# A hybrid attention kernel: the key copy moves to ScalarE, the value product of the next sequence moves behind the next pair's first value products

## The chip, the cores and the metric

One core of one Trainium2 chip. The metric is the device time of one execution in microseconds (us); the median of three runs stands for the kernel. Engines: PE (TensorE, matmuls), DVE (VectorE), ACT (ScalarE), POOL (GpSimd), SP (SyncE, which here only issues DMAs). Each runs its own list of instructions in the order written; they meet at semaphores.

## The reference

`x` is 8 sequences of 512 tokens by 128 features, float32. Four steps, each with a residual:

```
x = x + attention_a(layernorm(x))     # 16 heads of 64, causal softmax
x = x + ffn(layernorm(x))
x = x + attention_b(layernorm(x))     # 16 heads of 64, causal softmax, then
                                      # y = y_in + heads @ Wo; layernorm(y) * gamma + beta
x = x + ffn(layernorm(x))
ffn: s = x @ Win + bin; g = sum over 16 of relu(s*W1 + b1)*W2, + b2; g @ Wout + bout
```

## The kernel before

Three parts follow one another. The front runs attention a and the first ffn for each sequence. Then come the **heads** (attention b), with the **back** (residual, normalization with gamma and beta, second ffn) of earlier sequences woven in. A drain ends it. The change is in heads and back.

The heads run over 8 sequences b and, in each, 8 pairs of heads p: 64 pairs, numbered n = 8b + p. A pair has three units: unit 0 is query blocks 0 and 1, unit 1 is block 2, unit 2 is block 3 (each with the keys up to its own block). A pair's code has three steps s = 0, 1, 2, and in step s each engine does what is due:

- PE (`heads_tensor`, L890): the scores of unit s (L842, and the mask with L847) into one of two wide PSUM buffers; the value products of one unit of an earlier pair (`pair_values`, L867 to L869) into bank CT. Step 0 also: the query projection of the next pair into bank QK, and the output product of pair n-3 (L886). Step 1 also: the key projection of the next pair into the same bank QK, and `context_turn_tensor` (L872), the transposes of pair n-2's context into bank MB. Step 2 also: the back's products, and `values_tensor` (L780), which makes one eighth of the next sequence's values, again in bank MB.
- DVE (`heads_vector`, L959): the row maxima of unit s (L969); the conversion of an earlier unit's probabilities to f16 (`split_vector`, L957); in step 0 the reciprocals, the scaled context (L983) and `values_vector` (L797), which writes `v_lo`, what the f16 values leave over; in step 1 `keys_vector` (L824), the copy of the keys out of QK. Then one of the eight adds of the ffn (L1108, the first of them L1104), and the back's norms.
- ACT (`heads_scalar`, L917): the exponentials of unit s (L933); step 0: the query copy (L818); step 1: `ctx_t` (L943), the turned context out of MB; step 2: `values_scalar` (L793), which writes `v_hi`. One ReLU of the ffn per pair (L1189).
- POOL (`heads_gpsimd`, L1012): the low half of each unit's probabilities (L1018), and small parts of the back. SP issues the DMAs that transpose the probabilities.

What must wait for what, around the change:

- `context_turn_tensor` of pair n-2, run in pair n, overwrites MB, so it waits until `v_lo` has been written n + 8 times (L876). The first 8 are made before the heads; pair n adds one.
- `values_tensor` waits for `ctx_t`, for the same reason.
- Unit 0's scores wait for `q_sb` and `k_sb`; the next pair's query projection waits for `k_sb`.
- The back of sequence c runs in sequence b = c + 1 (residual sum and statistics at p = 2, centering at p = 3, residual at p = 4, the turn at p = 6, the product with Win at p = 7), its eight ReLUs and adds in sequence c + 2, and its output product (L1172) after them. The back of sequence 6 is drawn together after the last pair (b = 8).

Of the kernel before, what the change touches and what calls it, by code (L numbers as in the profile page):

```python
# [35 lines left out]
NU = len(UNIT_ROWS)  # L36
# [12 lines left out]
def hybrid_kernel(nc, x_in, a_wq, a_wk, a_wv, a_wo, b_wq, b_wk, b_wv, b_wo, gamma, beta,  # L49
                  f_win, f_bin, f_w1, f_b1, f_w2, f_b2, f_wout, f_bout, out):  # L50
    B, S, D = x_in.shape
# [12 lines left out]
    with ExitStack() as ctx:  # L64
# [660 lines left out]
        DRAIN = 2 * HP + 2  # L725
# [5 lines left out]
        def unit_of_ffn(b, p, s):  # L731

            if b == B:
                return p * NU + s if p < NU else None
            return p if s == 0 and 0 <= b - 2 < B else None

        def leaves(b, p):

            if b == B and p == 3:
                return B - 2  # L740
            return b - 3 if p == 0 and 0 <= b - 3 < B and b - 3 != B - 2 else None

        def pair_exists(b, p):

            return 0 <= HP * b + p < PAIRS
# [54 lines left out]
        def project_tensor(pe, b, p, parts, done):  # L800

            n = number(b, p)
            wait(pe, *(("k_sb", n) if done == "q_ps" else ("q_sb", n + 1)))
            if done == "q_ps" and p == 0:
                wait(pe, "g_xt", b - 1)
            if done == "q_ps" and p == 1:
                wait(pe, "g_s", b - 1)
            if done == "q_ps" and p == 2:
# [11 lines left out]
        def keys_vector(dve, b, p):  # L820
            n = number(b, p)
            wait(dve, "k_ps", n + 1)
            wait(dve, "s2", n - 1)
            dve.tensor_copy(k_sb[p % 2][:, :], QK).then_inc(sem("k_sb"), 1)  # L824
# [65 lines left out]
        def heads_tensor(pe, b, p):  # L890
            fresh = pair_exists(b, p)
            for s in range(NU):
                if fresh:
                    pair_scores(pe, b, p, s)
                old = earlier(b, p, 2 if s < LAG - NU else 1)
                if pair_exists(*old):
                    pair_values(pe, *old, (s - LAG) % NU)
                if s == 0:
                    if pair_exists(*later(b, p)):
                        project_tensor(pe, *later(b, p), wq_parts, "q_ps")  # L900
                    if pair_exists(*earlier(b, p, 3)):
# [12 lines left out]
                if s == 2 and b < B - 1:  # L914
                    values_tensor(pe, b, p)

        def heads_scalar(act, b, p):  # L917
            n = number(b, p)
            for s in range(NU):
                if s == 2 and p == 6 and 0 <= b - 1 < B:  # L920
                    back_xt_scalar(act, b - 1)
                if s == 2 and p == 7 and 0 <= b - 1 < B:
                    back_s_scalar(act, b - 1)
                if pair_exists(b, p):
# [34 lines left out]
        def heads_vector(dve, b, p):  # L959
            n = number(b, p)  # L960
            before = earlier(b, p, 1)
            for s in range(NU):
                if pair_exists(b, p):
# [7 lines left out]
                    last.then_inc(sem(f"m{s}"), 1)  # L971
                u = (s - 1) % NU
# [97 lines left out]
        def back_center_vector(dve, c, half):  # L1070
            wait(dve, "gy_mv", c + 1)
            for i in range(half * QB // 2, (half + 1) * QB // 2):
# [5 lines left out]
        def back_residual_vector(dve, c, half):  # L1078
            wait(dve, "g_c", 2 * c + 2)
            wait(dve, "gy_rstd", c + 1)  # L1080
            wait(dve, "x_beta", c + 1)
            wait(dve, "g_xb", c)
            for i in range(half * QB // 2, (half + 1) * QB // 2):
# [4 lines left out]

        def back_adds_vector(dve, b, p, s):

            if s == 0 and p == 0 and 0 <= b - 3 < B and b - 3 != B - 2:
                back_add_vector(dve, b - 3, J - 1)
            if b == B:
                j = unit_of_ffn(b, p, s)
                if j is not None and 0 < j <= J:
                    back_add_vector(dve, b - 2, j - 1)
            elif s == 0 and p > 0 and 0 <= b - 2 < B:
                back_add_vector(dve, b - 2, p - 1)
# [21 lines left out]
        def back_gpsimd(pool, b, p, u):  # L1120
# [3 lines left out]
            if p == 2 and u == 1:  # L1124
                wait(pool, "kept", 16 * B)
                wait(pool, "g_x", 2 * c)
# [5 lines left out]
            if p == 4 and u == 2:  # L1132
                wait(pool, "g_x", 2 * c + 2)
# [4 lines left out]
            if p == 5 and u == 0:  # L1138
# [3 lines left out]
            if p == 5 and u > 0:  # L1142
                if u == 1:
# [3 lines left out]
                for i in range((u - 1) * QB // 2, u * QB // 2):  # L1147
# [7 lines left out]
        def back_turn_tensor(pe, c):  # L1155
            wait(pe, "g_y", 2 * c + 2)
            wait(pe, "g_done", c if c == B - 1 else c - 1)
            wait(pe, "k_sb", bank_left(c + 1, 6))
            transposes(pe, QK, ffn_norm.tokens(), QB).then_inc(sem("g_xt_ps"), 1)

        def back_s_tensor(pe, c):
            wait(pe, "g_xt", c + 1)
            wait(pe, "k_sb", bank_left(c + 1, 7))
# [3 lines left out]
        def back_out_tensor(pe, c):  # L1167
            wait(pe, "g_add", J * c + J)
            wait(pe, "g_s", min(c + 2, B) if c != B - 2 else c + 1)
            wait(pe, "k_sb", bank_left(c + 3, 0))  # L1170
# [79 lines left out]
        def _(act):  # L1250
# [5 lines left out]
            queries_scalar(act, 0, 0)  # L1256
            over_pairs(act, heads_scalar)

        @block.vector
        def _(dve):  # L1260
# [5 lines left out]
            keys_vector(dve, 0, 0)  # L1266
# [26 lines left out]
```

## Time and profile before

| | |
|---|---|
| median of 3 runs | 909.11 us (909.02 to 909.72) |
| profiled execution | 910.46 us, span in the trace 908.7 us |
| heads, pairs 0 to 63 (trace) | from 239.15 us |
| granted PE clock, mean of the span | 0.919 of full speed |
| busy over the span | PE 81%, DVE 81%, ACT 60%, POOL 58% |

A busy time is the time in which an engine works on some instruction. Times in the trace count from the start of the span. What a change is worth is read inside the heads, from the start of one pair's scores on PE to the next one's.

### The profile page before, as it was taken

To read this page: it belongs to the slowest core of one execution; us is meant where nothing else is said; L and a number is where in the kernel's file an instruction comes from. 1 tells how busy PE (TensorE), PEld (TensorE's weight loads), DVE (VectorE), ACT (ScalarE), POOL (GpSimd) and SP (SyncE) were. 2 spreads that over 40 slices of the span, in tenths; PEclk is the share of its full clock that TensorE was granted. 3 is DMA by queue.
4 is the path that set the end of the run, shared out by engine and by line. 5 is a ranking of instruction groups with operands and counts; after the bars stand their busy time and mean duration, and the time that the engine had idled before them with its cause. 6 is when DMAs were issued, how large, how long until landed. Compare 5 with 4: busy or idle time off the path is not lost. (4 is left out here: it accounts for less than half of the span.)

```text
span 908.7 us, 21242 instructions
## 1 busy us (share of the span) xinstructions
PE 732.3 (81%) x7592; PEld 524.5 (58%) x7592; DVE 740.5 (81%) x1422; ACT 542.1 (60%) x1511; POOL 522.9 (58%) x496
## 2 busy tenths in 40 slices
PE   3476666641899999998899899889989998998852
PEld 2365555531557676675677567666756665675541
DVE  1478888864577789889989988998898899899973
ACT  0357666652466665675677567666756666765643
POOL 2146666443165666756756575676658566656831
PEclk9598878855799999999999999999999999999995
DMA  9111110101199987897789688888878887887740
GB/s 202 42 32 42 50 56 35 36 35 46 21 144 155 155 141 132 140 149 124 127 138 152 108 141 132 142 131 138 151 117 131 144 139 125 136 154 126 133 93 22
DMA packets 367142, 100.29 MB, mean 110 GB/s; under 512 B 347968, under 2 KB 364864, under 8 KB 367040
## 3 DMA queue, kind: packets, MB, share of 16 engines
q1 hardware_dynamic: 363776, 96.86, 61.6%
q10 hardware_dynamic: 3264, 2.10, 0.9%
q8 instruction: 60, 0.98, 0.5%
q14 instruction: 42, 0.34, 0.1%
HBM read 8.73 MB, written 2.10 MB: 12 GB/s over the span
## 5 line engine op out<-in xcount | busy, mean ns | idle before, releaser
L1018 POOL TENSOR_TENSOR prob_hl<-prob,prob_hl 128x768 f16<-128x768 f32 (+1 forms) x192 | 347.8, 1812 | 235.6 <-DVE prob_hl L957 235.6
L933 ACT ACTIVATE prob<-wide,neg_max 128x128 f32<-128x128 f32 (+3 forms) x512 | 264.5, 525 | 209.1 <-DVE neg_max L969 209.0
L969 DVE TENSOR_REDUCE neg_max<-wide 128x2 f32<-128x256 f32 (+3 forms) x256 | 203.6, 816 | 66.5 <-PE wide L847 65.0
L842 PE MATMUL wide<-k_sb,q_sb 64*128 64x128 f32 (+3 forms) x1024 | 190.8, 470 | 2.6 <-ACT prob L933 1.6
L867 PE MATMUL bank<-v_hi,prob_t 128*128 128x64 f16 x1280 | 132.2, 193 | 16.6 <-DMA prob_t<-prob_hl 8.8
L869 PE MATMUL bank<-v_hi,prob_t 128*128 128x64 f16 x1280 | 132.2, 193 | 0.0
L868 PE MATMUL bank<-v_lo,prob_t 128*128 128x64 f16 x1280 | 132.2, 193 | 0.0
L957 DVE CAST prob_hl<-prob 128x768 f16<-128x768 f32 (+1 forms) x192 | 126.4, 658 | 1.8 <-ACT prob L933 1.6
L867 PEld LDWEIGHTS bank<-v_hi,prob_t 128*128 128x128 f16 x1280 | 115.5, 98 | 20.5 <-issue 10.6
L869 PEld LDWEIGHTS bank<-v_hi,prob_t 128*128 128x128 f16 x1280 | 114.0, 98 | 0.0
L868 PEld LDWEIGHTS bank<-v_lo,prob_t 128*128 128x128 f16 x1280 | 113.8, 98 | 0.0
L933 ACT ACTIVATION_READ_ACCUMULATOR prob<-wide,neg_max 128x1 f32 x512 | 102.6, 200 | 0.0
L842 PEld LDWEIGHTS wide<-k_sb,q_sb 64*128 64x128 f32 x1024 | 72.4, 186 | 44.1 <-issue 35.7
L847 PEld LDWEIGHTS wide<-mask_bf,ident_bf 128*128 128x128 bf16 x512 | 29.1, 98 | 105.1 <-issue 105.1
L1108 DVE SCALAR_TENSOR_TENSOR ffn_g<-relu_two,w,ffn_g 128x512 f32<-128x512 f32 x56 | 87.6, 1563 | 1.8 <-ACT relu_two L1189 0.7
L886 PEld LDWEIGHTS bank<-wo_up,ctx_t 128*128 128x128 f32 x512 | 66.8, 191 | 6.1 <-ACT ctx_t L943 0.9
L886 PE MATMUL bank<-wo_up,ctx_t 128*128 128x128 f32 x512 | 67.7, 275 | 0.7 <-ACT ctx_t L943 0.7
L847 PE MATMUL wide<-mask_bf,ident_bf 128*128 128x128 bf16 x512 | 62.1, 224 | 0.0
L1189 ACT ACTIVATE relu_two<-ffn_s,b,w 128x512 f32<-128x512 f32 x64 | 52.7, 827 | 2.6 <-DVE ffn_g L1104 1.7
L410 ACT ACTIVATE v_hi<-ffn_s,b,w 128x512 f32<-128x512 f32 x64 | 51.2, 813 | 1.4 <-DVE ffn_g L417 0.4
L421 DVE SCALAR_TENSOR_TENSOR ffn_g<-v_hi,w,ffn_g 128x512 f32<-128x512 f32 x56 | 43.8, 783 | 5.6 <-ACT v_hi L410 4.2
L160 PE MATMUL bank<-wv_b_hi,xt_hi 128*128 128x512 f32 x62 | 32.5, 524 | 18.7 <-ACT ctx_t L943 16.6
(190 smaller groups left out, 1474.6 us busy)
## 6 DMA issues: line engine op xcount, KB each, us to landing
prob_t<-prob_hl SPq DMA_TRANSPOSE x384, 3.1
x_next<-in_L_attn_a_in_features SPq DMA_DIRECT2D x8, 256.0 KB, 3.1
x_attn<-in_L_attn_a_in_features SPq DMA_DIRECT2D x8, 256.0 KB, 3.0
x_sb<-x_done SPq DMA_DIRECT2D x8, 256.0 KB, 2.3
y_res<-bn_y SPq DMA_DIRECT2D x8, 256.0 KB, 2.3
out_x<-x_done SPq DMA_DIRECT2D x8, 256.0 KB, 2.7
wq_a<-in_L_attn_a_w_q ACTq DMA_DIRECT2D x1, 512.0 KB, 5.3
wq_b<-in_L_attn_b_Wq SPq DMA_DIRECT2D x1, 512.0 KB, 8.3
```

Source lines behind the costliest of these rows:

```text
L842: pe.matmul(dst[:, h, c:c + m], q[e, i * P:(i + 1) * P], k[e, 0:m], start=(i == UNIT_ROWS[u][0]), stop=False)
L847: last = pe.matmul(dst[:, h, c:c + P], ident_bf[:, :], mask_bf[:, :], start=False, stop=(i == UNIT_ROWS[u][-1]))
L867: pe.matmul(dst, prob_t[u][:, h * m + k, :], hi, start=(j == 0), stop=False)
L868: pe.matmul(dst, prob_t[u][:, h * m + k, :], lo, start=False, stop=False)
L869: last = pe.matmul(dst, prob_t[u][:, (2 + h) * m + k, :], hi, start=False, stop=(j == i))
L886: last = pe.matmul(YA[:, i * P:(i + 1) * P], ctx_t[:, i * P:(i + 1) * P], wo_up[:, p, :], start=(p == 0 and i == 0), stop=(p == HP - 1 and ...
L933: last = act.activation(prob_2[s][:, at:at + m], score_banks(p, s)[:, h, c:c + m], ACT.Exp, bias=neg_max[p % 2][:, h, i:i + 1], accum_out= ...
L957: dve.tensor_copy(prob_hl[u][:, 0:w], prob_2[u][:, 0:w]).then_inc(sem(f"ph{u}"), 1)
L969: last = dve.tensor_reduce(neg_max[p % 2][:, :, i:i + 1], score_banks(p, s)[:, :, c:c + m], AX.X, ALU.max, negate=True)
L1018: pool.tensor_tensor(prob_hl[u][:, w:2 * w], prob_2[u][:, 0:w], prob_hl[u][:, 0:w], ALU.subtract)\
L1108: dve.scalar_tensor_tensor(out=ffn_g[:, :], in0=relu_two[:, j % 2, :], scalar=w2_2[:, j:j + 1], in1=ffn_g[:, :], op0=ALU.mult, op1=ALU.add ...
L1189: act.activation(relu_two[:, j % 2, :], ffn_s[:, :], ACT.Relu, bias=b1_2[:, j:j + 1], scale=w1_2[:, j:j + 1]).then_inc(sem("g_relu"), 1)
```

## The change

Five things, all in heads and back.

1. `keys_vector` on DVE becomes `keys_scalar` on ACT, in step 1 behind the `ctx_t` copy.
2. `values_tensor` of pair n moves from the end of step 2 to step 0 of pair n+1, behind the first value products and before the query projection. `values_scalar` follows it to step 0 of pair n+1, behind the exponentials; `values_vector` goes from step 0 to step 1 of pair n+1, behind the conversion.
3. The ffn's ReLUs and adds move by one pair (the add of step 0 goes to step 1 of the next pair) and, on DVE, in front of the conversion.
4. Centering and residual aren't halved any more; each is done at once, in step 2 of p = 3 and p = 4, before the conversion. The statistics behind them, the moments and POOL's parts move back by one or more steps.
5. The turn, the product with Win and the output product of the back move back by one pair each, and the drain has one more pair.

```
-        DRAIN = 2 * HP + 2
+        DRAIN = 2 * HP + 3
...
+        def relu_at(b, p, s):
+
+            if b == B and p > 0:
+                k = (p - 1) * NU + s
+                return (B - 2, k) if k < J else None
+            c, j = (b - 2, p - 1) if p > 0 else (b - 3, J - 1)
+            return (c, j) if s == 0 and 0 <= c < B and c != B - 2 else None
+
+        def adds_at(b, p, s):
+
+            found = []
+            c, j = (b - 2, p - 2) if p > 1 else (b - 3, J - 2 + p)
+            if s == 1 and 0 <= c < B and c != B - 2:
+                found.append((c, j))
+            k = (p - 1) * NU + s
+            if b == B and 0 < k <= J:
+                found.append((B - 2, k - 1))
+            return found
...
-        def keys_vector(dve, b, p):
+        def keys_scalar(act, b, p):
             n = number(b, p)
-            wait(dve, "k_ps", n + 1)
-            wait(dve, "s2", n - 1)
-            dve.tensor_copy(k_sb[p % 2][:, :], QK).then_inc(sem("k_sb"), 1)
+            wait(act, "k_ps", n + 1)
+            wait(act, "s2", n - 1)
+            act.copy(k_sb[p % 2][:, :], QK).then_inc(sem("k_sb"), 1)
```

In `heads_tensor`:

```
                 if s == 0:
+                    bv, pv = earlier(b, p, 1)
+                    if 0 <= bv < B - 1:
+                        values_tensor(pe, bv, pv)
                     if pair_exists(*later(b, p)):
                         project_tensor(pe, *later(b, p), wq_parts, "q_ps")
...
-                if s == 2 and p == 6 and 0 <= b - 1 < B:
+                if s == 2 and p == 7 and 0 <= b - 1 < B:
                     back_turn_tensor(pe, b - 1)
-                if s == 2 and p == 7 and 0 <= b - 1 < B:
-                    back_s_tensor(pe, b - 1)
+                if s == 2 and p == 0 and 0 <= b - 2 < B:
+                    back_s_tensor(pe, b - 2)
                 if s == 2 and leaves(b, p) is not None:
                     back_out_tensor(pe, leaves(b, p))
-                if s == 2 and b < B - 1:
-                    values_tensor(pe, b, p)
```

In `heads_scalar`:

```
+                if s == 0:
+                    bv, pv = earlier(b, p, 1)
+                    if 0 <= bv < B - 1:
+                        values_scalar(act, bv + 1, pv, MB)
                 if s == 0 and pair_exists(*later(b, p)):
                     queries_scalar(act, *later(b, p))
                 if s == 1 and pair_exists(*earlier(b, p, 2)):
...
-                if s == 2 and b < B - 1:
-                    values_scalar(act, b + 1, p, MB)
-                j = unit_of_ffn(b, p, s)
-                if j is not None and j < J:
-                    back_relu_scalar(act, b - 2, j)
+                if s == 1 and pair_exists(*later(b, p)):
+                    keys_scalar(act, *later(b, p))
```

In `heads_vector`, behind the maxima:

```
+                for c, j in adds_at(b, p, s):
+                    back_add_vector(dve, c, j)
+                if s == 2 and p == 3 and 0 <= b - 1 < B:
+                    back_center_vector(dve, b - 1)
+                if s == 2 and p == 4 and 0 <= b - 1 < B:
+                    back_residual_vector(dve, b - 1)
                 u = (s - 1) % NU
                 if pair_exists(*(before if s == 0 else (b, p))):
                     split_vector(dve, *(before if s == 0 else (b, p)), u)
...
-                if s == 0:
+                if s == 1:
                     bv, pv = before
                     if 0 <= bv < B - 1:
                         values_vector(dve, bv + 1, pv, MB)
-                if s == 1 and pair_exists(*later(b, p)):
-                    keys_vector(dve, *later(b, p))
-                back_adds_vector(dve, b, p, s)
...
-                if s > 0 and p == 3 and 0 <= b - 1 < B:
-                    back_center_vector(dve, b - 1, s - 1)
-                if s < 2 and p == 4 and 0 <= b - 1 < B:
-                    back_residual_vector(dve, b - 1, s)
-                if s == 2 and p == 4 and 0 <= b - 1 < B:
-                    wait(dve, "g_x", 2 * b)
+                if s == 0 and p == 5 and 0 <= b - 1 < B:
+                    wait(dve, "g_x", b)
                     back_statistics(dve, ffn_norm, lambda i: x_ffn[:, i, :], "gf", b - 1)
-                if s == 0 and p == 5 and 0 <= b - 1 < B:
+                if s == 1 and p == 5 and 0 <= b - 1 < B:
                     back_moments(dve, ffn_norm, "gf", b - 1)
```

In `back_gpsimd` (POOL):

```
-            if p == 4 and u == 2:
-                wait(pool, "g_x", 2 * c + 2)
+            if p == 5 and u == 0:
+                wait(pool, "g_x", c + 1)
                 wait(pool, "g_done", c - 1)
...
-            if p == 5 and u == 0:
+            if p == 5 and u == 2:
                 back_rstd_gpsimd(pool, ffn_norm, "gf", c)
...
-            if p == 5 and u > 0:
-                if u == 1:
+            if p == 6 and u < 2:
+                if u == 0:
```

## Rows read from the trace of the kernel before

**Rows 1.** The page, busy us, share of the span and instructions of each engine.

```profile
PE 732.3 (81%) x7592; PEld 524.5 (58%) x7592; DVE 740.5 (81%) x1422; ACT 542.1 (60%) x1511; POOL 522.9 (58%) x496
```

**Rows 2.** Busy time by stretch: start:end, length, engines, PE clock, DMA share, GB/s.

```profile
282.69:291.62 8.93, 8.93 (x107) 6.30 (x106) 6.61 (x13) 5.84 (x19) 5.41 (x3) 1.00 0.98 146
465.30:546.26 80.96, 75.34 (x855) 52.57 (x854) 74.09 (x122) 53.42 (x163) 52.29 (x36) 1.00 0.80 134
584.82:596.62 11.80, 9.49 (x106) 6.43 (x105) 11.80 (x19) 6.55 (x20) 6.25 (x4) 1.00 0.71 113
798.28:856.28 58.00, 51.08 (x617) 36.00 (x617) 57.14 (x92) 36.28 (x114) 41.18 (x29) 1.00 0.82 136
856.28:908.70 52.42, 23.51 (x245) 16.95 (x244) 32.37 (x61) 23.08 (x44) 17.42 (x17) 0.74 0.35 69
```

**Rows 3.** Timeline of PE in pair 5: start us, us, instruction.

```profile
282.69 0.93 PE L842 MATMUL wide<-k_sb,q_sb 64*128 64x128 f32 x8
...
286.25 0.92 PE L842 MATMUL wide<-k_sb,q_sb 64*128 64x384 f32 x4
...
288.52 0.60 PE L194 MATMUL bank<-ident,ctx_sb 128*128 128x128 f32 x4
289.05 1.13 PE L842 MATMUL wide<-k_sb,q_sb 64*128 64x512 f32 x4
...
290.75 0.47 PE L160 MATMUL bank<-wv_b_hi,xt_hi 128*128 128x512 f32 x1
```

**Rows 4.** PE groups, 465.3 to 546.26: busy us, mean ns of one, idle before.

```profile
L1172 PE MATMUL bank<-wout,ffn_g 128*128 128x128 f32 x8 | 1.1, 285 | 0.0
L1164 PE MATMUL bank<-x_attn,win 128*128 128x512 f32 x2 | 1.1, 634 | 0.0
L194 PE MATMUL bank<-ident,fn_y 128*128 128x128 f32 x4 | 0.6, 279 | 0.7 <-DVE k_sb L824 0.7
```

**Rows 5.** PE's waits, 465.3 to 546.26: us in total, times, longest.

```profile
PE bank L160 <- ACT ctx_t L943: 3.2, 3, 1.4
PE bank L867 <- DVE ctx_sb L983: 1.0, 1, 1.0
```

**Rows 6.** Timeline of DVE in pair 5.

```profile
286.19 0.68 DVE L797 TENSOR_TENSOR v_lo<-bank,v_hi 128x512 f16<-128x512 f32 x1
287.42 0.96 DVE L969 TENSOR_REDUCE neg_max<-wide 128x2 f32<-128x768 f32 x1 [0.55 <-PE wide L847]
288.30 0.55 DVE L957 CAST prob_hl<-prob 128x768 f16<-128x768 f32 x1
288.76 0.69 DVE L824 COPY k_sb<-bank 128x512 f32<-128x512 f32 x1
...
291.57 0.55 DVE L957 CAST prob_hl<-prob 128x768 f16<-128x768 f32 x1
```

**Rows 7.** Timeline of ACT in pair 5.

```profile
288.41 0.58 ACT L933 ACTIVATE prob<-wide,neg_max 128x384 f32<-128x384 f32 x1 [1.16 <-DVE neg_max L969]
...
289.54 0.58 ACT L943 COPY ctx_t<-bank 128x512 f32<-128x512 f32 x1
```

**Rows 8.** Timeline of DVE, three of the ffn's adds and the instruction behind one.

```profile
611.65 2.22 DVE L1108 SCALAR_TENSOR_TENSOR ffn_g<-relu_two,w,ffn_g 128x512 f32<-128x512 f32 x1
...
631.32 1.58 DVE L1108 SCALAR_TENSOR_TENSOR ffn_g<-relu_two,w,ffn_g 128x512 f32<-128x512 f32 x1
...
881.11 0.74 DVE L1108 SCALAR_TENSOR_TENSOR ffn_g<-relu_two,w,ffn_g 128x512 f32<-128x512 f32 x1
881.77 0.87 DVE L1053 BATCH_NORM_STATS2 yn_stats<-y_res 128x6 f32<-128x128 f32 x4
```

**Rows 9.** Timeline of POOL beside the first two adds, and a unit of 768.

```profile
611.18 2.14 POOL L1018 TENSOR_TENSOR prob_hl<-prob,prob_hl 128x1024 f16<-128x1024 f32 x1
...
615.28 1.64 POOL L1018 TENSOR_TENSOR prob_hl<-prob,prob_hl 128x768 f16<-128x768 f32 x1 [0.67 <-DVE prob_hl L957]
...
630.22 2.14 POOL L1018 TENSOR_TENSOR prob_hl<-prob,prob_hl 128x1024 f16<-128x1024 f32 x1 [1.64 <-DVE prob_hl L957]
```

**Rows 10.** Timeline of PE, the start of pair 3.

```profile
264.84 0.93 PE L842 MATMUL wide<-k_sb,q_sb 64*128 64x128 f32 x8
```

More of the change, by code:

```diff
@@ L729, in hybrid_kernel @@
         y_norm = Norm("yn", ln_b_eps, applied=False)
[L731 to L735, printed above, removed]
+        def relu_at(b, p, s):
[13 more added lines that the diff above has]
+            return found
         def leaves(b, p):
-            if b == B and p == 3:
+            if b == B and p == 4:
                 return B - 2
-            return b - 3 if p == 0 and 0 <= b - 3 < B and b - 3 != B - 2 else None
+            return b - 3 if p == 1 and 0 <= b - 3 < B and b - 3 != B - 2 else None
         def pair_exists(b, p):
@@ L803, in project_tensor @@
             wait(pe, *(("k_sb", n) if done == "q_ps" else ("q_sb", n + 1)))
-            if done == "q_ps" and p == 0:
+            if done == "q_ps" and p == 1:
                 wait(pe, "g_xt", b - 1)
-            if done == "q_ps" and p == 1:
+            if done == "q_ps" and p == 2:
                 wait(pe, "g_s", b - 1)
-            if done == "q_ps" and p == 2:
+            if done == "q_ps" and p == 3:
                 wait(pe, "g_done", b - 2)
@@ L919, in heads_scalar @@
             for s in range(NU):
[L920 to L923, printed above, removed]
                 if pair_exists(b, p):
@@ L943, in heads_scalar @@
                     act.copy(ctx_t[:, :], MB[:, :]).then_inc(sem("ctx_t"), 1)
-                if s == 2 and b < B - 1:
-                    values_scalar(act, b + 1, p, MB)
-                j = unit_of_ffn(b, p, s)
-                if j is not None and j < J:
-                    back_relu_scalar(act, b - 2, j)
+                if s == 1 and pair_exists(*later(b, p)):
+                    keys_scalar(act, *later(b, p))
+                if s == 2 and p == 7 and 0 <= b - 1 < B:
+                    back_xt_scalar(act, b - 1)
+                if s == 2 and p == 0 and 0 <= b - 2 < B:
+                    back_s_scalar(act, b - 2)
+                if relu_at(b, p, s) is not None:
+                    back_relu_scalar(act, *relu_at(b, p, s))
         def split_vector(dve, b, p, u):
@@ L1068, in back_rstd_gpsimd, with back_center_vector @@
                 .then_inc(sem(f"{done}_rstd"), 1)
-        def back_center_vector(dve, c, half):
+        def back_center_vector(dve, c):
             wait(dve, "gy_mv", c + 1)
-            for i in range(half * QB // 2, (half + 1) * QB // 2):
+            for i in range(QB):
                 last = dve.scalar_tensor_tensor(out=y_gb[:, i, :], in0=y_res[:, c * QB + i, :],
@@ L1076, in back_center_vector, with back_residual_vector @@
             last.then_inc(sem("g_c"), 1)
-        def back_residual_vector(dve, c, half):
-            wait(dve, "g_c", 2 * c + 2)
+        def back_residual_vector(dve, c):
+            wait(dve, "g_c", c + 1)
             wait(dve, "gy_rstd", c + 1)
             wait(dve, "x_beta", c + 1)
-            wait(dve, "g_xb", c)
-            for i in range(half * QB // 2, (half + 1) * QB // 2):
+            wait(dve, "g_y", 2 * c)
+            for i in range(QB):
                 last = dve.scalar_tensor_tensor(out=x_ffn[:, i, :], in0=y_gb[:, i, :],
@@ L1087, in back_residual_vector @@
             last.then_inc(sem("g_x"), 1)
[L1089 to L1098, printed above, removed]
         def back_add_vector(dve, c, j):
@@ L1125, in back_gpsimd @@
                 wait(pool, "kept", 16 * B)
-                wait(pool, "g_x", 2 * c)
+                wait(pool, "g_x", c)
                 pool.tensor_tensor(x_beta[:, :, :], x_sb[:, seq(c), :],
@@ L1146, in back_gpsimd @@
                     wait(pool, "g_xt_ps", c)
-                for i in range((u - 1) * QB // 2, u * QB // 2):
+                for i in range(u * QB // 2, (u + 1) * QB // 2):
                     last = pool.tensor_scalar(ffn_norm.y[:, i, :], x_ffn[:, i, :], ffn_norm.neg_mean[:, i:i + 1],
@@ L1157, in back_turn_tensor @@
             wait(pe, "g_done", c if c == B - 1 else c - 1)
-            wait(pe, "k_sb", bank_left(c + 1, 6))
+            wait(pe, "k_sb", bank_left(c + 1, 7))
             transposes(pe, QK, ffn_norm.tokens(), QB).then_inc(sem("g_xt_ps"), 1)
@@ L1162, in back_s_tensor @@
             wait(pe, "g_xt", c + 1)
-            wait(pe, "k_sb", bank_left(c + 1, 7))
+            wait(pe, "k_sb", bank_left(c + 2, 0))
             pe.matmul(QK[:, :], win2[:, :, :].rearrange("p a m -> p (a m)"), ffn_xt, start=True, stop=True)\
@@ L1168, in back_out_tensor @@
             wait(pe, "g_add", J * c + J)
+            wait(pe, "g_done", c)
             wait(pe, "g_s", min(c + 2, B) if c != B - 2 else c + 1)
-            wait(pe, "k_sb", bank_left(c + 3, 0))
+            wait(pe, "k_sb", bank_left(c + 3, 1))
             for i in range(QB):
@@ L1256, in _ @@
             queries_scalar(act, 0, 0)
+            keys_scalar(act, 0, 0)
             over_pairs(act, heads_scalar)
@@ L1265, in _ @@
                 values_vector(dve, 0, k, VB[k % len(VB)])
-            keys_vector(dve, 0, 0)
             over_pairs(dve, heads_vector)
```

## Prediction

> **What bounds the kernel now.** I read the page's busy shares first. PE and DVE are level at 81% of the span, ACT and POOL far below [rows 1]. That leaves open which one sets the time, so I cut the heads part (B) into stretches. Pair 5 lasts 8.93 us, PE is busy for all of it and DVE for only 6.61. A whole sequence in the middle (pairs 24 to 31) lasts 80.96, with PE 75.34 and DVE 74.09; pair 36 alone lasts 11.80, with DVE busy for all of it and PE for 9.49 [rows 2]. So there are two regimes: PE sets the time where DVE has only the pair's own work, and DVE sets it where a normalization of the back part falls.
>
> How much each is worth comes from PE's own order. Pair 5 starts at 282.69, pair 6 at 291.62, with no gap [rows 2, 3]: 8.93 us is PE's floor for a pair that also makes a value product. Eight of them are 71.4 us. The three back-end products of a sequence take 0.6, 1.1 and 1.1 us [rows 4], about 0.2 of each overlapping its neighbours: 2.3 us. The remaining 80.96 - 71.4 - 2.3 = 7.3 us per sequence are waits, the largest of them PE's wait for `ctx_t` (3.2), behind which DVE's lateness stands [rows 5].
>
> **What a pair looks like on PE.** Call T the start of unit 1's scores, 286.25. The context turn starts at T+2.27, unit 2's scores at T+2.80, the value product at T+4.50, and the next pair at T+5.37; so the value product costs 0.87 [rows 2, 3]. On DVE the maximum of unit 1 starts at T+1.17, the conversion of unit 0 at T+2.05, and the instruction behind it (now the key copy) at T+2.51 [rows 6].
>
> **Part 1: the key copy goes from DVE to ACT.** DVE loses 0.69 us per pair, 0.6 of which counts, because starts overlap the end before by 0.08. ACT gains a copy of 0.58 [rows 6, 7]. ACT is busy for 53.42 of 80.96 [rows 2], so it has the room. Its order matters more: the copy stands behind unit 1's exponentials (T+2.16) and the `ctx_t` copy (T+3.29) [rows 7]. Without any other wait it ends at about T+3.29+0.46+0.58 = T+4.33; the next scores start at T+4.50 now that the value product isn't before them. Cost nothing, with a cover of 0.2 us.
>
> **Part 2: the value product goes from the end of pair n to step 0 of pair n+1.** PE's work is the same. The wait for `ctx_t` that stood in front of it is now met long before it. But the product writes bank MB, and the context turn of step 1 writes MB too. The turn waits for `v_lo` number n + 8, which is the second half of exactly this product: DVE must have subtracted it before PE may turn. Before, that subtraction was in DVE's step 0, over at 286.87 [rows 6], 1.65 us ahead of the turn (288.52). The diff moves it to step 1, behind the maximum of unit 1, the add and the conversion of unit 0.
>
> So a new chain closes inside each pair: unit 1's scores, maximum, add, conversion, `v_lo`, turn. Without an add, `v_lo` takes the slot of the key copy: it starts at T+2.51, takes 0.68 [rows 6], ends at T+3.19, and PE resumes some 0.03 later, at T+3.22 in place of T+2.27. Stall: **0.95 us**. Unit 1's maximum can't start earlier, because it waits for PE. Behind the turn PE has unit 2's scores, and then everything up to the next unit 1, all in order, so nothing gives the stall back. DVE was the late one before and has no fault here: even when it is free, the chain is longer than PE's 2.27.
>
> **Part 3: the adds.** From sequence 2 on each pair has one add, now between maximum and conversion, so it lengthens the same chain. What it costs there must be chosen. In its place of now it takes 1.58 or 2.22 [rows 8]. Both times it ends 0.54 us after the POOL subtraction that runs beside it (630.22+2.14 = 632.36 against 632.90; 611.18+2.14 = 613.32 against 613.87) [rows 8, 9]. It stands still while POOL works. With POOL idle it takes 0.74, and the next instruction starts after 0.66 [rows 8]. Is POOL idle at the new place? The conversion of unit 1 ends at 291.57+0.55, 3.07 after unit 2's scores start (289.05); the next pair S starts 1.70 after those scores, so that is S+1.37 [rows 3, 6]. POOL's subtraction (1.64) runs to S+3.06; a conversion of unit 2 held back until then ends some 0.55 later, and POOL's 2.14 for unit 2 are over by about S+5.8 [rows 9]. The add comes at T+2.05 with T = S+3.56+0.87, so at S+6.5. It clears POOL by 0.7 us. I take 0.66: the stall is 0.95 + 0.66 = **1.61 us**. The other end is 1.58, a stall of 2.45.
>
> **Part 4: center and residual in one piece each, statistics and moments a step later.** They stay on DVE, which now has 0.6 us less per pair for the key copy, 0.8 less for the add and a longer pair. I cost them at nothing on DVE. They do push POOL's work later, so that in three or four pairs of eight POOL still runs when the add comes. By the rows of the add this is 0.3 to 0.8 us each time; I take 1.2 us per sequence, 6 in all (bounds 0 and 16).
>
> **The sum.** Pairs 3 to 56 last from 264.84 to 798.28, 533.4 us [rows 2, 10]. PE's floor in them is 53 x 8.93 + 8.06 (pair 56 makes no value product) = 481.4, the back-end products 12.4; waits 39.6, and these go. Pair 56 gains a value product (+0.87), one output product leaves the stretch (-0.9). Stalls: pairs 3 to 17, 15 x 0.95 = 14.3; pairs 18 to 56, 39 x 1.61 = 62.8. Together -39.6 + 77.1 = **+37.5**. Pairs 0 to 2: one stall more, one value product less, +0.1. POOL in the way: +6. Pairs 57 to 62 have no value product and no stall; they last 58.00, DVE 57.14 of it [rows 2], while PE needs 6 x 8.06 + 0.9 = 49.3. DVE is relieved, but in pairs this short the cover of 0.2 us for the key copy goes with each late maximum: I take 3 us for that, **-5.7** (bounds -8.7 and -3). Tail (52.42 [rows 2]): the turn of the last sequence moves in (+0.5), and the eight ReLUs of sequence 6 start one pair later, so their adds stand ahead of the last sequence's centering: **+3** (bounds 0 and 5). Sum: 37.5 + 0.1 + 6 - 5.7 + 3 = +40.9. The profiled execution took 910.46 and would take 951.4; the median of the runs is 909.11, so I forecast **950 us**.
>
> **Rivals.**
> 1. *DVE was the bound and its relief decides: faster.* For it: DVE is busy for 92% of a sequence (74.09 of 80.96) and PE loads weights for 52.57, 65% [rows 2]. If PE had room for the stall, the 39.6 us of waits and most of the 8.7 in the last pairs would go and nothing come back: about 865. Against it: pair 5 leaves PE no gap, and DVE's 6.61 don't explain its length. The point of decision is the stall: 39.6 + 5.7 over 55 pairs is 0.8 us; below that the kernel is faster. That needs `v_lo` by T+3.0, and without any add it comes at T+3.19. The Trainium skill (Perfetto Trace Analysis, Identifying the Most-Contended Engine) says that matmul busy time is no good measure for PE and that LDWEIGHTS busy is to be used; by it PE has a third of its time free and this rival would hold. I trust the gap-free pair more.
> 2. *The adds still run into POOL in every pair.* Then 39 x 0.84 = 33 us more: about 983. It needs POOL to be 0.7 us later than I worked out.
> 3. *The stall overlaps waits that I let vanish*, or is shorter because PE refills faster behind it: 915 to 934.
>
> **Chances.** Forecast's case (934 to 968) 0.78; rival 1 0.06; rival 2 0.08; rival 3 0.06; within 0.2%, what a measurement of this kernel can't tell from no change, 0.02. The low end of the range, 934, has no POOL cost, -8.7 in pairs 57 to 62 and nothing in the tail (938), and a stall shorter by 0.07. The high end, 970, has POOL's 16, -3, and 5 (966), and a stall longer by 0.07. Faster 0.06, same 0.02, slower 0.92.
>
> **What would show it.** In the profile after: pair 5 lasts 9.9 us and a middle pair 10.5 to 11, where both regimes were before; PE waits for `v_lo` in front of the context turn, 1 us without an add and 1.6 with one, 55 times, and no more for `ctx_t`; the add takes 0.75 in most pairs; DVE is busy for some 62 us of a sequence of 86. Pairs from 57 on last 8.1 to 9. Wrong would be: a turn that doesn't wait, adds of 1.6, or PE gaps before unit 0's scores (the key copy late on ACT).

## The result

The changed kernel takes 965.53 us (median of 4 runs, 964.21 to 967.33) against 909.07 for the kernel before: a ratio of 1.062 (95% interval 1.060 to 1.064). It is slower by 56 us; forecast were 950, with 934 to 970 as the range.

**The profile after.** The page's busy shares answer to [rows 1]:

```profile
PE 742.8 (77%) x7592; PEld 531.4 (55%) x7592; DVE 655.5 (68%) x1358; ACT 579.6 (60%) x1575; POOL 517.6 (54%) x496
```

DVE is relieved by 85 us, and the kernel is slower all the same. The stretches, in the columns of [rows 2]: pair 5, two pairs of sequence 3 (p = 4 and p = 5), pairs 32 to 39, pairs 57 to 62, the tail.

```profile
283.27:293.22 9.95, 9.05 (x108) 6.36 (x105) 6.62 (x11) 6.45 (x20) 5.42 (x3) 1.00 0.72 140
526.44:537.39 10.95, 9.36 (x109) 6.43 (x106) 8.71 (x16) 7.04 (x21) 5.43 (x3) 1.00 0.67 129
537.39:550.08 12.69, 10.91 (x108) 7.10 (x105) 9.69 (x24) 7.15 (x21) 6.64 (x4) 0.87 0.69 119
571.77:662.71 90.94, 78.15 (x856) 54.39 (x855) 60.78 (x115) 58.23 (x170) 51.47 (x35) 0.96 0.66 121
853.48:907.44 53.96, 51.13 (x621) 36.36 (x621) 44.34 (x86) 40.05 (x121) 37.84 (x25) 1.00 0.90 145
907.44:963.40 55.96, 25.38 (x251) 18.84 (x248) 34.04 (x62) 24.11 (x45) 20.17 (x21) 0.72 0.33 62
```

Pair 5 was 8.93 us with PE busy throughout; now it is 9.95 with PE busy for 9.05. A sequence was 80.96 with DVE busy for 74.09; now it is 90.94 with DVE busy for 60.78. Pairs 57 to 62, which have no value product, got shorter as a stretch (58.00 before). No engine is full, and that is the sign of a chain that runs over several engines. The granted clock, 1.00 before from pair 1 to the end of the heads, is below that in some pairs now (0.87 in the third row).

The chain itself, PE and then DVE in pair 5 (timeline):

```profile
287.52 0.92 PE L855 MATMUL wide<-k_sb,q_sb 64*128 64x384 f32 x4
...
290.86 0.63 PE L194 MATMUL bank<-ident,ctx_sb 128*128 128x128 f32 x4 [0.90 <-DVE v_lo L810]
291.42 1.13 PE L855 MATMUL wide<-k_sb,q_sb 64*128 64x512 f32 x4
```

```profile
288.69 0.96 DVE L986 TENSOR_REDUCE neg_max<-wide 128x2 f32<-128x768 f32 x1 [1.21 <-PE wide L860]
289.57 0.55 DVE L974 CAST prob_hl<-prob 128x768 f16<-128x768 f32 x1
290.04 0.68 DVE L810 TENSOR_TENSOR v_lo<-bank,v_hi 128x512 f16<-128x512 f32 x1
292.80 1.23 DVE L986 TENSOR_REDUCE neg_max<-wide 128x2 f32<-128x1024 f32 x1 [2.09 <-PE wide L860]
```

With T = 287.52: the maximum starts at T+1.17, `v_lo` at T+2.52 and ends at T+3.20, as in the prediction (T+1.17, T+2.51, T+3.19). The turn starts at T+3.34, not T+3.22: PE took 0.14 us to resume behind DVE, not the 0.03 that the forecast put there. DVE then sits idle for 2.09 us, waiting for PE. Neither engine is full: each waits for the other in every pair.

PE's waits from 263.39 to 853.48 (pairs 3 to 56), in all:

```profile
PE bank L194 <- DVE v_lo L810: 76.6, 54, 1.8
PE bank L880 <- DMA prob_t<-prob_hl: 0.3, 1, 0.3
```

54 waits in 54 pairs and hardly anything else; the wait for `ctx_t` of [rows 5] is gone. The adds, 571.77 to 662.71:

```profile
L1113 DVE SCALAR_TENSOR_TENSOR ffn_g<-relu_two,w,ffn_g 128x512 f32<-128x512 f32 x7 | 5.5, 784 | 0.0
```

They take 0.78 us on the average, against 1.81 in the same pairs before. That is a mean: 0.74 in most pairs, 1.05 where POOL still runs beside the add (p = 3).

### The profile page after: what moved, and what is told of

The parts are those of the page before. It is cut to its first block and busy times, and to the rows that moved or that the text cites. A ratio compares the mean times of both kernels' runs of the same rounds, so it can differ in the third digit from the quotient of the medians.

```text
span 963.4 us, 21234 instructions
## 1 busy us (share of the span) xinstructions
PE 742.8 (77%) x7592; PEld 531.4 (55%) x7592; DVE 655.5 (68%) x1358; ACT 579.6 (60%) x1575; POOL 517.6 (54%) x496
## 5 line engine op out<-in xcount | busy, mean ns | idle before, releaser
L855 PE MATMUL wide<-k_sb,q_sb 64*128 64x128 f32 (+3 forms) x1024 | 195.7, 481 | 0.9 <-ACT k_sb L837 0.8
L880 PE MATMUL bank<-v_hi,prob_t 128*128 128x64 f16 x1280 | 135.4, 195 | 9.5 <-DMA prob_t<-prob_hl 8.6
L974 DVE CAST prob_hl<-prob 128x768 f16<-128x768 f32 (+1 forms) x192 | 141.6, 738 | 1.0 <-DMA prob_t<-prob_hl 0.7
L881 PE MATMUL bank<-v_lo,prob_t 128*128 128x64 f16 x1280 | 135.3, 195 | 0.0
L882 PE MATMUL bank<-v_hi,prob_t 128*128 128x64 f16 x1280 | 135.3, 195 | 0.0
L880 PEld LDWEIGHTS bank<-v_hi,prob_t 128*128 128x128 f16 x1280 | 117.7, 99 | 13.4 <-issue 10.7
L881 PEld LDWEIGHTS bank<-v_lo,prob_t 128*128 128x128 f16 x1280 | 115.9, 99 | 0.1
L882 PEld LDWEIGHTS bank<-v_hi,prob_t 128*128 128x128 f16 x1280 | 115.9, 99 | 0.0
L194 PE MATMUL bank<-ident,ctx_sb 128*128 128x128 f32 x256 | 40.1, 279 | 76.7 <-DVE v_lo L810 76.6
L194 PEld LDWEIGHTS bank<-ident,ctx_sb 128*128 128x128 f32 x256 | 27.3, 141 | 100.0 <-issue 99.1
L957 ACT COPY ctx_t<-bank 128x512 f32<-128x512 f32 x64 | 37.5, 585 | 66.7 <-PE bank L194 66.5
```

The source lines that it names most:

```text
L194: last = pe.transpose(dst[:, k * P:(k + 1) * P], src[:, k * P:(k + 1) * P], ident[:, :])
L855: pe.matmul(dst[:, h, c:c + m], q[e, i * P:(i + 1) * P], k[e, 0:m], start=(i == UNIT_ROWS[u][0]), stop=False)
L880: pe.matmul(dst, prob_t[u][:, h * m + k, :], hi, start=(j == 0), stop=False)
L881: pe.matmul(dst, prob_t[u][:, h * m + k, :], lo, start=False, stop=False)
L882: last = pe.matmul(dst, prob_t[u][:, (2 + h) * m + k, :], hi, start=False, stop=(j == i))
L974: dve.tensor_copy(prob_hl[u][:, 0:w], prob_2[u][:, 0:w]).then_inc(sem(f"ph{u}"), 1)
```

## The experiments

All times are medians. Where a kernel was timed in rounds, its ratio to the kernel before on the same chip stands with its interval; the others (e2, e3, e6, e7, e11) are single runs beside 908 to 914 us for the kernel before. The runs of one kernel lie 3 to 6 us apart, so a single run is good to about that. In each diff the context lines are those of the kernel that the experiment starts from, and ... stands for lines left out.

### How long the chain is, and how long the kernel takes

**e1: `v_lo` back in step 0** (from the changed kernel).

```
-                if s == 1:
+                if s == 0:
                     bv, pv = before
                     if 0 <= bv < B - 1:
                         values_vector(dve, bv + 1, pv, MB)
```

> The changed kernel with one thing undone: v_lo stays in DVE's step 0, behind the scaled context, where it was before the change. Theory A (the whole loss is PE's wait for v_lo in front of the context turn): the wait is gone, since v_hi is written about 4.4 us into the pair and v_lo ends near 5.1, while the turn comes at about 6.7; a pair lasts 8.9 to 9.0 us, the granted PE clock stays at 1.00 in the heads, and the time falls below that of the kernel before, to 870 to 885 us. Rival B (the new order of PE's work, or the key copy on ACT, costs the time): it stays above 930. Rival C (DVE then waits for v_hi in step 0 and hands the lateness to the maximum of unit 1): 895 to 930, with waits of PE for k_sb or for exponentials.

884.72 us, ratio 0.972 (0.968 to 0.975). One digit takes back 81 us and leaves a kernel that is 2.8% faster than the one before. The sequence at 533.02:

```profile
533.02:609.81 76.79, 74.03 (x855) 53.17 (x854) 63.61 (x115) 57.42 (x170) 52.86 (x36) 1.00 0.86 144
```

76.79 us where the floor of PE is 71.4 + 2.3 = 73.7, and in the whole trace PE never waits for `v_lo`. Theory A holds; rivals B and C fall. What makes this kernel faster than the one before is another question, taken up behind e12.

**e2: `v_lo` in step 1, directly behind the maximum.**

```
+                if s == 1:
+                    bv, pv = before
+                    if 0 <= bv < B - 1:
+                        values_vector(dve, bv + 1, pv, MB)
                 for c, j in adds_at(b, p, s):
                     back_add_vector(dve, c, j)
...
-                if s == 1:
-                    bv, pv = before
-                    if 0 <= bv < B - 1:
-                        values_vector(dve, bv + 1, pv, MB)
```

> The changed kernel with v_lo in step 1 directly behind unit 1's maximum, in front of the add and the conversion. Theory A: the chain is scores, maximum, v_lo only; the wait in front of the turn is 0.5 us in all 55 pairs, with or without an add, and a pair lasts 9.45 us; 903 to 915 us in all. Rival B: no change beside the changed kernel, above 955. It says whether the loss scales with what stands in front of v_lo.

908.92 us, as forecast; the waits are 49, of 0.45 us on the average.

**e3: the adds behind `v_lo`.**

```
-                for c, j in adds_at(b, p, s):
-                    back_add_vector(dve, c, j)
...
                         values_vector(dve, bv + 1, pv, MB)
+                for c, j in adds_at(b, p, s):
+                    back_add_vector(dve, c, j)
```

> The changed kernel with the ffn's adds behind v_lo in step 1, nothing else moved. Theory A: the wait in front of the turn is 1.0 us in all pairs (it was 1.66 where an add stands); 39 pairs x 0.66 = 26 us less, and 3 to 7 less for the drops of the granted clock, so 932 to 940 us. If the adds weren't part of the chain: about 965.

936.12 us, as forecast.

**e11: one more conversion in the chain.**

```
+        spare = sb("spare", [P, 768], F16)
...
+            if u == 0:
+                wait(dve, "again", n)
+                dve.tensor_copy(spare[:, :], prob_2[u][:, 0:w]).then_inc(sem("again"), 1)
             dve.tensor_copy(prob_hl[u][:, 0:w], prob_2[u][:, 0:w]).then_inc(sem(f"ph{u}"), 1)
```

> The changed kernel with 0.46 us more in the chain: in step 1 DVE also converts unit 0's probabilities into a spare tile, in front of the real conversion. It computes the same. Theory A: the wait in front of the turn grows by 0.46 in each of 55 pairs (1.46 without an add, 2.1 with one), 25 us, so 991 us if the granted clock of PE does as in the changed kernel (six drops to 1.2 GHz of 3.4 us, 1.3 us of loss each). Theory K (longer waits bring more such drops): twenty or more drops, 20 to 35 us on top, 1005 to 1025 us. If the chain isn't the cause: 966 to 975.

1015.63 us, within what theory K gave and 25 us above theory A alone. The row of the wait in front of the turn, over the whole span, for e2, e3 and e11:

```profile
PE bank L194 <- DVE v_lo L810: 21.9, 49, 0.7
```

```profile
PE bank L194 <- DVE v_lo L810: 52.3, 54, 1.2
```

```profile
PE bank L194 <- DVE v_lo L811: 101.6, 55, 2.3
```

| kernel | what stands in front of `v_lo` in step 1 | wait, us | time, us | time - e1 |
|---|---|---|---|---|
| e1 | (step 0) | 0 | 884.7 | 0 |
| e2 | maximum | 21.9 | 908.9 | 24.2 |
| e3 | maximum, conversion | 52.3 | 936.1 | 51.4 |
| changed | maximum, add, conversion | 76.6 | 965.5 | 80.8 |
| e11 | maximum, add, two conversions | 101.6 | 1015.6 | 130.9 |

In e2 and e3, whose clock stays at full speed in the heads, the loss is the wait within 2.5 us. The changed kernel has six falls of the clock in its heads as well, worth 8 us (below); that 80.8 is still near 76.6 is because e1 has other waits that are mostly gone in it (14.4 us for transposed probabilities in its heads, against 4.3). From the changed kernel to e11 the waits grow by 25.0 us and the time by 50.1. The other 25 go with the granted clock: e11's heads have 24 falls, 18 more than the changed kernel's, and 18 x 1.4 us is 25. The stretch 400 to 800 of e3, of the changed kernel and of e11:

```profile
400.00:800.00 400.00, 360.84 (x4078) 250.26 (x4075) 334.01 (x549) 278.44 (x813) 250.85 (x168) 1.00 0.75 131
```

```profile
400.00:800.00 400.00, 343.70 (x3806) 237.84 (x3802) 271.03 (x507) 258.36 (x754) 226.28 (x154) 0.97 0.68 121
```

```profile
400.00:800.00 400.00, 333.66 (x3487) 229.66 (x3486) 263.12 (x497) 238.74 (x699) 209.15 (x143) 0.92 0.62 111
```

In this stretch the clock of e3 is at 2.4 GHz all the time; that of the changed kernel is at 1.2 GHz for some of it, and that of e11 for more (a mean of 0.92 is 16% of the time at half speed).

### The parts alone, on the kernel before

**e7: only `v_lo` to step 1.**

```
-                if s == 0:
+                if s == 1:
                     bv, pv = before
                     if 0 <= bv < B - 1:
                         values_vector(dve, bv + 1, pv, MB)
```

> The kernel before with one edit: v_lo goes from step 0 to step 1 of the same pair, behind the conversion. The value product, the key copy and the adds stay. Theory A: this alone makes the loss. Pairs without an add last 9.9 us (8.93 and a wait of 0.95 to 1.0 in front of the turn); with an add, which stays in step 0 and runs into POOL, the maximum is late too, up to 1.9 us of wait; 945 to 985 us. Rival (the move of the value product is needed for the loss): below 925.

1013.75 us. The sign and the mechanism were right; the size lies 29 us beyond the upper bound of 985. Pairs without an add last 10.0 us, near the forecast of 9.9. For the pairs with one: a sequence's stretch, its adds, and the wait in front of the turn over the whole span:

```profile
592.29:690.98 98.69, 81.61 (x856) 54.94 (x855) 77.80 (x122) 54.23 (x164) 51.54 (x36) 0.93 0.62 111
```

```profile
L1108 DVE SCALAR_TENSOR_TENSOR ffn_g<-relu_two,w,ffn_g 128x512 f32<-128x512 f32 x7 | 15.8, 2252 | 0.0
```

```profile
PE bank L194 <- DVE v_lo L797: 96.6, 54, 2.9
```

The adds, in step 0, take 2.25 us on the average and hold up the maximum, so the wait reaches 2.9 us, and the clock's mean is 0.93. So the place of `v_lo` makes a loss by itself; the product needn't move for it. Of the 48 us that e7 takes beyond the changed kernel, 20.0 are the longer wait (96.6 against 76.6), and its more frequent falls of the clock are worth some 20 more (an estimate, at 1.4 us a fall). That the changed kernel is spared them by its new place for the adds fits the rows, but it wasn't tried by itself.

**e8: only the value product and `v_hi` to step 0 of the next pair.**

```
                 if s == 0:
+                    bv, pv = earlier(b, p, 1)
+                    if 0 <= bv < B - 1:
+                        values_tensor(pe, bv, pv)
...
-                if s == 2 and b < B - 1:
-                    values_tensor(pe, b, p)
...
+                if s == 0:
+                    bv, pv = earlier(b, p, 1)
+                    if 0 <= bv < B - 1:
+                        values_scalar(act, bv + 1, pv, MB)
...
-                if s == 2 and b < B - 1:
-                    values_scalar(act, b + 1, p, MB)
```

> The kernel before with one part: the value product and v_hi move to step 0 of the next pair, v_lo stays in step 0. Keys stay on DVE, adds where they were. Theory A: no new wait; PE's waits for ctx_t (3.2 us per sequence) go, part of DVE's lateness stays in the pairs with the normalization: 888 to 905 us. Rival (moving the product costs by itself, since v_hi comes later than v_lo could start): 909 or more.

916.31 us, ratio 1.006 (1.004 to 1.008): a miss, slower where 888 to 905 was expected. PE's waits from 400 to 750:

```profile
PE wide L842 <- ACT prob L934: 8.2, 9, 1.2
PE bank L867 <- DVE ctx_sb L986: 6.7, 5, 1.6
PE bank L867 <- DMA prob_t<-prob_hl: 5.8, 6, 2.0
PE bank L160 <- ACT q_sb L818: 5.3, 12, 0.8
```

The waits for `ctx_t` (14.4 us in the same stretch before) are gone, but others have come: for the exponentials, for `q_sb` (now behind `v_hi` on ACT) and for the transposed probabilities. In the pairs with the normalization DVE is still late, and that its lateness comes out in these waits is my reading; it wasn't tried. The granted clock fell as well (mean 0.98 in this stretch). In two pairs (p = 7 of sequences 4 and 5) PE waits 2.0 us at a time for transposed probabilities and the clock is down behind it; they last 13.4 and 13.5 us where the other sequences' last 10.3 to 10.4. These two alone are 6 us in the profiled run, the size of the loss.

**e9: only the adds to step 1, in front of the conversion.**

```
-                back_adds_vector(dve, b, p, s)
...
+                back_adds_vector(dve, b, p, s)
                 u = (s - 1) % NU
...
-            elif s == 0 and p > 0 and 0 <= b - 2 < B:
+            elif s == 1 and p > 0 and 0 <= b - 2 < B:
```

> The kernel before with one part: the adds go from the end of step 0 to step 1, in front of the conversion, with the ReLUs where they were. e6 gave 29 us for this place in the changed order, and there it was the start of the add against POOL's subtraction. Theory L: DVE loses about 0.8 us per pair with an add; PE's waits per sequence (7.3 us) shrink to 1 to 3: 880 to 895 us. Rival (the gain needs the moved value product, because PE's wait for ctx_t stays): 898 to 909 us.

898.36 us, ratio 0.986 (0.983 to 0.989), 3 us outside what theory L gave and at the edge of the rival. The rival's reason doesn't hold: over 300 to 800 PE's waits for `ctx_t` went from 16.6 us to 2.4. Part of that came back as waits for `ctx_sb` (5.9 before, 9.6 now) and for transposed probabilities (3.7, and none before). The adds of the sequence at 540.34 take 1.16 us on the average, not 0.74 and not 1.81; four of them take 0.74, and where POOL runs beside them they take up to 2.4:

```profile
L1108 DVE SCALAR_TENSOR_TENSOR ffn_g<-relu_two,w,ffn_g 128x512 f32<-128x512 f32 x7 | 8.1, 1159 | 0.0
```

**e4: only the key copy to ACT.**

```
                     act.copy(ctx_t[:, :], MB[:, :]).then_inc(sem("ctx_t"), 1)
+                if s == 1 and pair_exists(*later(b, p)):
+                    keys_scalar(act, *later(b, p))
...
-                if s == 1 and pair_exists(*later(b, p)):
-                    keys_vector(dve, *later(b, p))
```

> The kernel before with the key copy moved to ACT, behind the ctx_t copy, and nothing else. DVE loses 0.6 us per pair; that counts in the pairs where DVE sets the time (four or five of eight), about 3 us per sequence, so 888 to 896 us. If the copy on ACT makes k_sb late or takes the time of the exponentials of unit 2, the gain shrinks: 900 to 912 us, with waits of PE for k_sb.

921.04 us, ratio 1.011 (1.008 to 1.013): a miss, beyond both ranges. PE's waits from 300 to 800:

```profile
PE bank L160 <- ACT ctx_t L943: 15.3, 16, 1.3
PE bank L194 <- ACT k_sb L824: 9.1, 5, 1.8
...
PE bank L1164 <- ACT k_sb L824: 3.2, 5, 0.7
PE bank L1172 <- ACT k_sb L824: 2.8, 4, 0.7
```

The back's three products share bank QK with the keys, and so they wait for the copy, which on ACT stands behind the exponentials and `ctx_t`: 15.1 us of waits for `k_sb`, where the kernel before has 3.6 in the same stretch. The `ctx_t` wait stayed (16.6 before).

### The other parts, on e1

**e5: the key copy back on DVE.**

```
-            act.copy(k_sb[p % 2][:, :], QK).then_inc(sem("k_sb"), 1)
+            dve.tensor_copy(k_sb[p % 2][:, :], QK).then_inc(sem("k_sb"), 1)
...
-                if s == 1 and pair_exists(*later(b, p)):
-                    keys_scalar(act, *later(b, p))
...
+                if s == 1 and pair_exists(*later(b, p)):
+                    keys_vector(dve, *later(b, p))
```

> The kernel of e1 (v_lo in step 0) with the key copy back on DVE, in step 1 behind the conversion, as before the change. Theory A: the key copy's place isn't what cost or what gained the time; DVE has room in most pairs (busy 80%), so 880 to 895 us. If moving the key copy is what made e1 fast (relief of DVE), it goes back to 900 or more. If the copy on ACT was late for the next scores (its cover was 0.2 us), this one is faster than e1: below 882.

884.74 us, ratio 0.971 (0.969 to 0.974), the same as e1. In this order the key copy's engine is worth nothing.

**e6: the adds in step 0, behind `v_lo`.**

```
-            if s == 1 and 0 <= c < B and c != B - 2:
+            if s == 0 and 0 <= c < B and c != B - 2:
...
                         values_vector(dve, bv + 1, pv, MB)
+                for c, j in (adds_at(b, p, s) if s == 0 else []):
+                    back_add_vector(dve, c, j)
```

> The kernel of e1 with the adds in step 0, behind v_lo, in place of step 1. Theory L (an add stands still until POOL's subtraction is over, and then takes 0.54): the add starts near 5.1 us into the pair, POOL works until about 5.8, the add takes 1.2 to 1.3 us in place of 0.74 and unit 1's maximum comes 0.5 to 0.7 late: 39 pairs make 20 to 27 us, so 903 to 912 us. If adds cost 0.74 in any place: 885 us as e1.

914.04 us, 29 more than e1 and 2 beyond the forecast. One sequence's adds, e6 (542.39 to 625.33) and e1 (533.02 to 609.81):

```profile
L1115 DVE SCALAR_TENSOR_TENSOR ffn_g<-relu_two,w,ffn_g 128x512 f32<-128x512 f32 x7 | 7.7, 1107 | 0.0
```

```profile
L1113 DVE SCALAR_TENSOR_TENSOR ffn_g<-relu_two,w,ffn_g 128x512 f32<-128x512 f32 x7 | 5.2, 742 | 0.0
```

The longer adds are only half of it: 39 x 0.365 = 14 us. In the pairs p = 0 and p = 1 the add takes 0.74 here too, but with `v_lo` it stands in front of unit 1's maximum, which starts at T+1.60 and not at T+1.17. A late maximum makes the exponentials late and, behind them on ACT, the key copy, for which PE then waits; e1 has 1.7 us of this wait in its heads:

```profile
PE wide L855 <- ACT k_sb L837: 24.2, 15, 2.1
```

Here the thin cover of part 1 does run out. The clock falls five times in the heads of this kernel and never in those of e1; at 1.4 us a fall, 7 us, that covers the 2 us beyond the forecast.

**e10: e1 with the moments of p = 3, the statistics and the moments of p = 5 one step later.**

```
-                if s == 0 and p == 3 and 0 <= b - 1 < B:
+                if s == 1 and p == 3 and 0 <= b - 1 < B:
                     back_moments(dve, y_norm, "gy", b - 1)
-                if s == 0 and p == 5 and 0 <= b - 1 < B:
+                if s == 1 and p == 5 and 0 <= b - 1 < B:
                     wait(dve, "g_x", b)
...
-                if s == 1 and p == 5 and 0 <= b - 1 < B:
+                if s == 2 and p == 5 and 0 <= b - 1 < B:
                     back_moments(dve, ffn_norm, "gf", b - 1)
```

> The kernel of e1 with three small pieces of the norms moved out of step 0: moments of the first norm to step 1 of p = 3, statistics of the second to step 1 and its moments to step 2 of p = 5. In e1 the pairs p = 3 and p = 5 last 9.4 and 10.0 us, with PE waiting for k_sb 0.5 to 1.0, since unit 1's maximum stands behind these pieces. Theory A: 0.5 and 0.8 us less per sequence: 876 to 881 us. If the pieces only push the lateness to step 2: 884 as e1.

878.77 us, ratio 0.966 (0.963 to 0.970), as forecast: its four runs (878.14 to 881.89) lie below all four of e1 (882.69 to 887.85). It has the lowest median of this study; a sequence takes 75.5 us.

**e12: e10 with the key copy on DVE** (the edit of e5).

```
-            act.copy(k_sb[p % 2][:, :], QK).then_inc(sem("k_sb"), 1)
+            dve.tensor_copy(k_sb[p % 2][:, :], QK).then_inc(sem("k_sb"), 1)
...
```

> The kernel of e10 with the key copy back on DVE, as in e5. In e5 the copy's place made no difference (884.7 against 884.7 us), but e10 still shows PE waiting for k_sb in p = 3 and p = 5 (0.3 us each), and the copy on DVE doesn't stand behind the exponentials. If that wait is all that is left of the copy's cost: 876 to 879 us. If DVE, which then has 0.6 us more per pair, is late in p = 4 to p = 6: 879 to 885 us.

882.38 us, ratio 0.968 (0.967 to 0.970). It lies in the range of the second case (DVE late), but its interval and e10's overlap; the two aren't told apart.

**What makes e1 faster than the kernel before (885 against 909) is not shown.** e5, which has the key copy where it was, is as fast as e1, so it isn't that copy. The adds alone gave 11 us (e9), the value product alone cost 6 (e8), and the places of centering, residual, statistics and the back's products (points 4 and 5 of the change) were never tried by themselves.

## Why the prediction was right, point by point

**The bound.** PE's floor of 8.93 us per pair held within 0.07 (the gap-free pairs of e1, with the new order, last 8.86): e10 gets within 2 us per sequence of 73.7, and with DVE busy for 62 of 75.5 us. Rival 1 (DVE is the bound, PE has room) would have given 865; it was wrong, and with it the reading by weight loads. The Trainium skill (Perfetto Trace Analysis, Identifying the Most-Contended Engine) has PE's headroom judged by MFU (the share of the peak matmul rate) and LDWEIGHTS busy. The trace doesn't agree on the second: LDWEIGHTS was busy for 65% of a sequence and 70% of pair 5 [rows 2], with not one gap to use. MFU wasn't worked out.

**Part 2, the new chain.** Right in mechanism and place, and shown from both sides: e1 takes it away, e2 and e3 shorten it, e11 lengthens it, e7 makes it alone.

**Part 3, the adds.** 0.74 us with POOL idle was the right choice for most pairs (0.78 on the average in the sequence shown), not the 1.58 of their old place; rival 2 did not occur. The add clears POOL by 0.5 us where 0.7 was worked out: in pair 54 POOL's subtraction ends at T+1.54 and the add starts at T+2.05.

**Part 1, the key copy.** Costed at nothing, measured as nothing in e5. That this needs the new order and an early maximum I hadn't said: e6 has 24 us of waits for `k_sb`, and on the kernel before the move costs 1.1% (e4). There ACT copies the back's turn out in front of unit 2's exponentials, and in the changed kernel behind them and one pair later; whether that is what makes the key copy free was not tried.

**The sum.** By stretch, in the profiled executions (910.46 and 965.30, 54.8 us apart, of which 0.1 lies outside the span):

| stretch | forecast | measured |
|---|---|---|
| up to pair 3 | +0.1 | -1.5 |
| pairs 3 to 56 | +43.5 | +56.7 (590.1 against 533.4) |
| pairs 57 to 62 | -5.7 | -4.0 |
| tail | +3 | +3.5 |
| sum | +40.9 | +54.7 |

The term that was mis-sized is the middle one, by 13 us, and two things make nearly all of it. First, the stall per pair: 9.95 against 8.93 us is 1.02, not 0.95, and 10.61 (p = 6) is 1.68, not 1.61. PE resumes 0.14 us behind DVE and not 0.03; some of that 0.11 comes back, as the rest of the pair is a little shorter in the new order. 54 x 0.07 = 4 us. Second, what I hadn't in the sum at all: the granted clock. The pair p = 5 takes 12.69 us at a mean clock of 0.87 (the third of the rows by stretch) and 11.14 in sequence 6 at 1.00. Six places in the heads lose 1.2 to 1.6 us in that way against the same pairs of other sequences, some 8 us. In the pair of 12.69 the scores of unit 2 show it:

```profile
546.16 0.76 PE L194 MATMUL bank<-ident,ctx_sb 128*128 128x128 f32 x4 [1.77 <-DVE v_lo L810]
546.86 2.08 PE L855 MATMUL wide<-k_sb,q_sb 64*128 64x512 f32 x4
```

2.08 us for what took 1.13 at 291.42: 1.2 in place of 2.4 GHz, right behind a wait of 1.77 us.

**Part 4, center, residual, statistics.** The 6 us that I put down for POOL came out at 5 (pairs p = 3, 4, 5 are 0.3, 0.3 and 0.5 us above p = 6, p = 2 is 0.2 below), but not all of it is POOL. In p = 3 and p = 4 the add does run beside POOL's subtraction and takes 1.05 and 1.07 us. In p = 5 it takes 0.74; what is late is the maximum, which starts at T+1.72 in place of T+1.17 (T = 813.36 in sequence 6), behind the statistics of the second norm:

```profile
814.30 0.86 DVE L1069 BATCH_NORM_STATS2 fn_stats<-x_ffn 128x6 f32<-128x128 f32 x4
815.08 0.94 DVE L986 TENSOR_REDUCE neg_max<-wide 128x2 f32<-128x768 f32 x1
```

So "nothing on DVE" was wrong by 0.5 us in each of six sequences, and part of that size was luck. The same pairs of sequence 1, which has no adds yet, are 0.4 to 0.5 us longer too.

**The range.** Without the clock's 8 us the changed kernel would have taken some 957. The clock is no term of the sum or of the range; that the result of 965.5 still lies below 970 is owed to the 16 us allowed for POOL. The two ends don't start from the same number either: the high end adds up from 951.4, the low end from 950, and from 950 the high end is 969. Two of the signs were missed: pairs 57 to 62 last 8.2 to 9.9 us, not 8.1 to 9, and a sequence lasts 90, not 86.

## What to carry to other kernels

When an instruction moves past others, list who waits for its result and through which buffer: here a subtraction of 0.68 us went 3 us later on an engine with room to spare, and the tensor engine, which had none, waited for it in each pair, since both work on one PSUM bank. Read the bound pair by pair: the average (81% and 81%) didn't say which engine set the time, one gap-free pair did. When work moves to another engine, look whether its new place is early enough for those who share its buffers: in e4 it wasn't.

## What the runs showed of the hardware

- **The clock fell in the kernels with the longer waits.** From 400 to 800 us, with waits of up to 1.2 us in every pair (e3) the granted clock is 1.00; with waits of up to 1.8 (the changed kernel) it is 0.97; with up to 2.3 (e11) 0.92, and 25 us are lost beyond the longer wait. A fall to 1.2 GHz costs 1.2 to 1.6 us here. The kernel before, with waits of up to 1.4 us now and then, had 1.00, and e8, where single waits reach 2.0 us, 0.98. What decides is left open.
- **An add with both inputs in SBUF stands still beside POOL's subtraction**: the same add takes 0.74, 1.11, 1.16, 1.81 or 2.25 us in e1, e6, e9, before and e7, as means over a sequence, by how many of them meet POOL. The Trainium skill (SBUF — State Buffer, Who interferes with whom) calls this an exclusive lock on a port pair that VectorE and GpSimd share, held for a whole instruction; the ends in [rows 8, 9] agree with it.
- **A conversion is held up too.** In pair 11 (p = 3 of sequence 1) the conversion of unit 0 runs beside POOL's subtraction and takes 0.92 us, and 0.55 in the pair before it; the pair is 0.37 us longer.
- **DVE's time freed isn't time saved.** The key copy off DVE (0.6 us per pair) made the kernel before slower (e4), and DVE 85 us less busy went with 56 us more in the changed kernel.
